# One-bank maxima, half-length value passes, a split first group, column gates, more work on POOL and a new step table in an adaLN attention block

## The reference

```python
mod = (silu(c) @ wmod)              # six vectors of 128: sa, ca, ga, sb, cb, gb
ga, gb = sign(ga) * max(|ga|, 0.25), sign(gb) * max(|gb|, 0.25)
h = layernorm(x) * (1 + ca) + sa
q, k, v = h @ Wq.T, h @ Wk.T, h @ Wv.T          # 8 heads of 16
probs = softmax(causal(q @ k.T / 4))
x = x + ga * (probs @ v)
h = layernorm(x) * (1 + cb) + sb
p = softmax(h @ gate_W.T)                       # 8 experts
scale = count(p > 0.3) * p                      # counts fall on experts 0 and 1
x = x + gb * ((sum over experts of scale * (h @ expert_W.T)) @ out_W.T)
```

## Time and profile before

| what | value |
|---|---|
| runs of the kernel before | 287.44, 288.61, 291.89 us |
| median | 288.61 us |
| time of the profiled execution | 290.65 us |
| its span, first to last instruction | 288.9 us |
| mean granted clock of TensorE | 0.892 of full speed |

### The profile page before, as it was taken

The page is one execution under the profiler, slowest core; times in us unless marked ns, Lnnn a source line. Parts: engine busy times, 40 slices in busy tenths (PEclk is TensorE's granted clock), DMA queues, the critical chain, the costliest instruction groups (busy, mean ns, idle before and its releaser), DMA issues.

```text
span 288.9 us, 6404 instructions
## 1 busy us (share of the span) xinstructions
PE 274.0 (95%) x2427; PEld 168.8 (58%) x2427; DVE 214.7 (74%) x435; ACT 194.6 (67%) x415; POOL 38.9 (13%) x72
## 2 busy tenths in 40 slices
PE   6999999989999999999999999999999999999944
PEld 2656564546564535446686766676666666666622
DVE  3769999798699979999996499997686863704033
ACT  2344576455499668859986348786768899989910
POOL 7510004002032102000110000200110101101000
PEclk9799996895799979999975599986979999899995
DMA  7200000000000000100000010000000000000000
GB/s 196 59 1 2 0 5 1 5 0 2 2 0 3 3 3 0 37 2 1 2 5 0 0 39 2 2 3 19 2 2 1 3 23 0 2 1 5 20 0 18
DMA packets 5583, 3.42 MB, mean 12 GB/s; under 512 B 457, under 2 KB 5393, under 8 KB 5553
## 3 DMA queue, kind: packets, MB, share of 16 engines
q1 hardware_dynamic: 4976, 2.50, 3.2%
q10 hardware_dynamic: 576, 0.53, 0.6%
HBM read 1.84 MB, written 1.05 MB: 10 GB/s over the span
## 4 chain that ended last, share of the span: by engine, by line
PE 68%; DVE 13%; issue 9%; ACT 6%; DMA 2%; ACTq 1%; POOL 0%; POOLq 0%; DVEq 0%
PE ctx_ps L981 18%; PE ps L944 15%; PE ps L957 14%; DVE part_max L732 10%; PE ps L996 5%; ACT probs L631 3%; PE ps L1061 3%; PE ps L965 2%; PE ps L1030 2%; DMA w_sb<-in_L_attn_Wk 2%; PE ps L1043 2%; PE ps L1050 1%; PE ps L1056 1%; PE ps L1036 1%; PE ps L1025 1%
## 5 line engine op out<-in xcount | busy, mean ns | idle before, releaser
L732 DVE TENSOR_REDUCE part_max<-ps 128x2 f32<-128x1024 f32 (+3 forms) x160 | 163.3, 1060 | 28.0 <-PE ps L965 16.0
L631 ACT ACTIVATE probs<-ps 128x512 f32<-128x512 f32 x208 | 104.1, 607 | 27.4 <-PE ps L944 26.9
L944 PE MATMUL ps<-q_stack,k_stack 50*128 50x256 f32 (+3 forms) x512 | 88.0, 337 | 0.8 <-ACT probs L631 0.2
L957 PE MATMUL ps<-k_stack,q_stack 48*128 48x512 f32 (+3 forms) x320 | 80.1, 465 | 2.0 <-DVE part_max L732 0.6
L944 PEld LDWEIGHTS ps<-q_stack,k_stack 50*128 50x128 f32 x512 | 63.0, 199 | 25.6 <-ACT probs L631 7.4
L981 PE MATMUL ctx_ps<-probs,v_aug 128*32 128x256 f32 (+3 forms) x1024 | 73.5, 427 | 0.0
L957 PEld LDWEIGHTS ps<-k_stack,q_stack 48*128 48x128 f32 x320 | 38.1, 199 | 24.4 <-DVE part_max L732 9.6
L628 ACT ACTIVATE probs<-ps 128x512 f32<-128x512 f32 (+3 forms) x96 | 40.4, 499 | 17.3 <-PE ps L944 16.9
L981 PEld LDWEIGHTS ctx_ps<-probs,v_aug 128*32 128x32 f32 x1024 | 30.7, 115 | 28.1 <-issue 9.9
L602 POOL TENSOR_SCALAR_AFFINE_SELECT probs<-probs 128x512 f32<-128x512 f32 x32 | 20.2, 635 | 169.6 <-ACT probs L631 99.3
L996 PE MATMUL ps<-piece,spread 128*128 128x512 f32 x64 | 23.0, 476 | 0.0
(11 more groups left out here) (91 smaller groups left out, 171.5 us busy)
## 6 DMA issues: line engine op xcount, KB each, us to landing
x_sb<-in_L_attn_hidden_states SPq DMA_DIRECT2D x4, 256.0 KB, 5.3
out_x<-result SPq DMA_DIRECT2D x2, 256.0 KB, 2.5
out_x<-result SPq DMA_DIRECT2D x4, 128.0 KB, 1.8
wmod<-in_L_wmod ACTq DMA_DIRECT2D x1, 384.0 KB, 5.0
q_stack<-max_row SPq DMA_DIRECT2D x16, 4.0 KB
expert_w<-in_L_ffn_expert_W SPq DMA_DIRECT2D x1, 128.0 KB, 5.5
q_stack<-max_row SPq DMA_DIRECT2D x8, 8.0 KB
w_sb<-in_L_attn_Wv SPq DMA_DIRECT2D x1, 64.0 KB
```

The source lines that it names most:

```text
L631: drained(act.activation(probs[:, :, prob_columns(b)].rearrange("p (n e) q -> p e n q", e=2)[:, e], bank.rearrange("p (n q) -> p n q", n=2 ...
L732: dve.tensor_reduce(part_max[:, n % 2, i, 2 * e:2 * e + 2, c], banks[:, :, 0:width], AX.X, ALU.max).then_inc(vec_drained, 1)
L944: last = pe.matmul(out_at, k_stack[at:at + rows, p, j * P:(j + 1) * P], q_stack[at:at + rows, p, tile * P + q0:(tile + tiles) * P], start= ...
L957: last = pe.matmul(banks[:, m, 0:width], q_stack[at:at + ROWS, p, tile * P:(tile + 1) * P], k_stack[at:at + ROWS, p, c * BANK:c * BANK + w ...
```

## The change

Seven things change together.

- `maxima`: a unit is now one bank. On chunks wider than 256 keys a unit is one head (matmul, then its two masks on the diagonal, then a reduction of 512 columns at most); on narrower ones it is two heads that share a half of the rows, side by side in one bank. The units alternate between the halves. 160 units become 288: 256 of one head and 32 of two. `PAIR_STAGES` holds the ffn alone.
- `PASS_UNITS` goes from 4 to 2: 76 passes in place of 40.
- `GROUPS`: the first group of 512 tokens becomes two of 256; there are five groups, with 40 spreads in place of 32. The loads are split and ordered anew: x in pieces of 256 tokens first, the modulation's first two vectors ahead of the other four, Wk on the SP queue, and the weights of values and experts last.
- Gates as columns: the modulation's gates are computed as columns of one element for each partition. POOL scales the rows of Wv and out_W by them before they are transposed (`scale_weights`, `gated_weights`), in place of DVE work on 128x256 elements. ACT copies the product of the experts' weights out (`expert_out`).
- More on POOL: the normalized tiles that ACT made, the add of the variance's epsilon, `context_add` of items 0 to 9, and for the last three groups both pieces of the projections (`project_wide`: ACT copies the bank to `wide`, POOL makes the high piece and the low one).
- `WARM` goes from (11, 1, 2, 8) to (8, 1, 2). `bn`, `mean_var`, `var_eps` and `rstd` have a place for each norm in place of two that alternate.
- `ORDER` is a new table of 905 letters for 725, with two new streams (T the statistics of a group, V values and gates).

The core of the diff:

```diff
-NG = S // GROUP
+GROUPS = [(0, 2), (2, 2), (4, 4), (8, 4), (12, 4)]
+SPLIT_GROUPS = 2
-PASS_UNITS = 4
-WARM = (11, 1, 2, 8)
+PASS_UNITS = 2
+WARM = (8, 1, 2)
...
-    return [("maxima", n, i, e, c) for i in range(BLOCKS[n // 2][1]) for e in range(HALF // 2)
-            for c in range(key_chunks(n))]
+    units = []
+    for i in range(BLOCKS[n // 2][1]):
+        for c in range(key_chunks(n)):
+            narrow = maxima_width(n, i, c) <= BANK // 2
+            units += [("maxima", n, i, heads, c) for heads in ([(0, 2), (1, 3)] if narrow else [(0,), (1,), (2,), (3,)])]
+    return units
...
+def by_vec_norm(s):
+    return s in (("normalize", 0), ("normalize", 1), ("normalize2", NB - 1))
+def by_vec_add(n):
+    return n >= NI - 2
...
+                    for t in range(tiles):
+                        pool.tensor_scalar(normed[:, k % 2, t, :], x_sb[:, first + t, :], mean_var[:, k, t, 0:1],
+                                           rstd[:, k, t:t + 1], ALU.subtract, ALU.mult).then_inc(pool_normed, 1)
+                elif step[0] == "project_wide":
...
+                    pool.tensor_copy(piece[0][:, g % 2, qk, :], wide[:, qk, :]).then_inc(pool_pieces, 1)
+                    pool.wait_ge(pool_pieces, pieces_until(g, qk) - 1)
+                    pool.tensor_tensor(piece[1][:, g % 2, qk, :], wide[:, qk, :], piece[0][:, g % 2, qk, :].bitcast(F32),
+                                       ALU.subtract).then_inc(pool_pieces, 1)
+                elif step[0] == "context_add" and not by_vec_add(step[1]):
...
+                    pool.tensor_tensor(part, part, ctx_norm[:, n % 2, 0:tiles, :], ALU.add).then_inc(x_added, 1)
...
+                elif step[0] == "scale_weights":
+                    pool.wait_ge(gates_ready, 1)
+                    pool.wait_ge(ffn_in, 16 * 3)
+                    for k in range(2):
+                        pool.tensor_scalar(w_sb[:, 2 + k, :], w_sb[:, 2 + k, :], gates[:, k:k + 1], None,
+                                           ALU.mult).then_inc(weights_scaled, 1)
...
-                    dve.tensor_reduce(part_max[:, n % 2, i, 2 * e:2 * e + 2, c], banks[:, :, 0:width], AX.X,
+                    dve.tensor_reduce(part_max[:, n % 2, i, heads[0]:heads[-1] + 1:2, c],
+                                      banks[:, 0, 0:len(heads) * width].rearrange("p (e k) -> p e k", k=width), AX.X,
                                       ALU.max).then_inc(vec_drained, 1)
...
-                    for m in range(2):
-                        p, at = pair_of(n, 2 * e + m)
-                        last = pe.matmul(banks[:, m, 0:width], q_stack[at:at + ROWS, p, tile * P:(tile + 1) * P],
-                                         k_stack[at:at + ROWS, p, c * BANK:c * BANK + width],
-                                         start=True, stop=c < g)
-                    if c == g:
-                        pe.wait_ge(const_ready, CONSTS["halves"])
-                        for half in range(2):
-                            for m in range(2):
-                                at = TILE * m
-                                last = pe.matmul(banks[:, m, width - P:width], ident_half[at:at + TILE, half, :],
-                                                 mask_half[at:at + TILE, half, :], start=False, stop=half == 1)
+                    for m, e in enumerate(heads):
+                        p, at = pair_of(n, e)
...
+                        last = pe.matmul(banks[:, 0, m * width:(m + 1) * width],
+                                         q_stack[at:at + ROWS, p, tile * P:(tile + 1) * P],
+                                         k_stack[at:at + ROWS, p, c * BANK:c * BANK + width],
+                                         start=True, stop=c < diagonal_chunk)
+                        if c == diagonal_chunk:
+                            pe.wait_ge(const_ready, CONSTS["halves"])
+                            for half in range(2):
+                                last = pe.matmul(banks[:, 0, (m + 1) * width - P:(m + 1) * width],
+                                                 ident_half[at:at + TILE, half, :], mask_half[at:at + TILE, half, :],
+                                                 start=False, stop=half == 1)
...
 ORDER = (
-    "AAAAMAMMMMAMMMAXXAAAMMMMMXMAAMMAAAAMXMMMMAMMAXAAMXSMAASMSMASSSSSMSMSSASSMSAMXMPMSSXAMMXMMAAMSMAAMMMS"
+    "TTAAVTMTMMMVTAAAAAAAAAVAAMMMMAAMMMMXVAXATXMMMMMMVXAMTMMMMMVAAAMMXSSAMMXSTMMXMSSASSMMXMSSMMMSPSMMSSSP"
```

More of the change, by code:

```diff
@@ L148, in key_chunks, with group_of, groups_between, columns @@
     return BLOCKS[n // 2][0] // TG + 1
[L151 to L153 removed]
+def group_of(tile):
+    return [g for g, (first, tiles) in enumerate(GROUPS) if first <= tile < first + tiles][0]
+def groups_between(first, last):
+    return range(group_of(first), group_of(last) + 1)
+def columns(g):
+    first, tiles = GROUPS[g]
+    return slice(first * P, (first + tiles) * P)
+def maxima_units(n):
+    units = []
[4 more added lines that the diff above has]
+    return units
 def token_stats(name, k):
```

475 lines of the change are left out of this document (264 added, 211 removed).

## The result

| what | before | after |
|---|---|---|
| median (runs) | 288.02 us (4) | 256.67 us (4) |
| lowest to highest | 286.74 to 291.89 | 256.57 to 257.73 |
| profiled execution, span | 290.65, 288.9 | 256.59, 254.9 |
| granted clock | 0.892 | 0.985 |

The kernel before, and some experiments on it, have slower executions beside the usual ones; ratios and intervals leave these out, while medians are over all executions.

The account below looks back on a forecast made before the run. It saw successive limits: start, DVE (19 to 145 us), PE (to 235), ACT (to 276.5). Gains 5.5 + 2 + 0 + 2 = 9.5 off 290.65 gave 281.1, a median of 279 us; range 266 to 294.

Parts of the forecast that it names:

- The start: 0 to 19 us: earlier weights, shorter path, half widths and fewer zero matmuls bring the first maximum about 5.5 us earlier (3 to 8).
- DVE is busy 114.82 of 126: it bounds, and PE waits for banks: Reading of the profile before, 19 to 145 us: DVE is the limit there and PE waits for its banks.
- I take 2 us of it back, between 0 and 8: 19 to 145 us: of 11.2 us in which DVE idles, single banks were to recover 2 us.
- some 13 us of lost column time, of which I take 3 back, with 0 and 8 as bounds: 145 to 235 us: loss from a clock of 0.85; buffers freed sooner were to recover 3 us.
- my two stages: 19 to 145 us, taken as bound by DVE, gain 2 us; 145 to 235 us, taken as bound by PE, gain 0.
- The rival that I called much faster: Single banks remove most waiting and the clock at 145 to 235 us rises to 0.96: 263 us (262 to 273), chance 0.19.
- Changes of mode: PE: 41 more switches between scores and values at 0.245 us, 10 us in all, 3.5 of it at 145 to 235 us.
- Masks in order: PE diagonals: the second head starts only with the first one's last mask; up to 10 us, taken as 2.5.
- The split of a reduction: DVE maxima: 128 more instructions at 0.07 us each cost 9.0 us, paid for by work moved off DVE.
- POOL: POOL's busy time rises from 38.9 to 54 to 123 us; it doesn't bound, so the added work is costed at 0.
- The part of ACT: 235 to 276.5 us, bound by ACT: six normalized tiles of the last blocks leave ACT, 2 us gained.
- the sign that I named for it: ACT busy for fewer than 38 us in the last 41 would show that the normalized tiles leaving it paid.

Follow-up runs that it names:

- a_late: Changed kernel with 14 more matmuls on zeros ahead of the first projection, first maximum 2.4 us later: 260.53 us, ratio 0.9133.
- b_half: Kernel before with each maxima reduction reading only half of its columns: 284.95 us, ratio 0.9646.
- b_fill128all: Kernel before with two 128-column matmuls on zeros ahead of each maxima unit of all 12 items, 8.5 us of work: 283.46 us, ratio 0.9866.
- a_pair: Changed kernel with maxima units in aligned pairs of banks again, table otherwise kept: 283.99 us, ratio 0.9805.
- a_pass4: Changed kernel with PASS_UNITS 4 in place of 2, 50 fewer changes between rows and columns: 276.58 us, ratio 0.9603.
- a_pass3: Changed kernel with PASS_UNITS 3 in place of 2, 62 passes for 76: 267.98 us, ratio 0.9352.
- a_interleave: Changed kernel with the masks of two neighbouring diagonal units behind both matmuls, alternating as before, at 53 places: 256.84 us, ratio 0.9011.
- a_dve: Changed kernel with the adds to x and all normalized tiles back on DVE: 266.20 us, ratio 0.9331.
- b_onebank: Kernel before with one-bank maxima units alone, its own table kept with each M repeated per part: 300.81 us, ratio 1.0313.
- b_newtable: Kernel before with the new order table alone, translated to its steps: 338.12 us.
- a_oldtable: Changed kernel with the old order table translated to its steps and `expert_out` computed earlier: 320.21 us.
- b_fill: Kernel before with two 512-column matmuls on zeros ahead of each maxima unit of items 0 to 5: 290.34 us, ratio 1.0076.
- b_fill128: Kernel before with two 128-column matmuls on zeros ahead of each maxima unit of items 0 to 5, 3.8 us of work: 288.99 us, ratio 1.0028.

## Why the prediction was wrong

The start was right. I gave 5.5 and it is 6.1, the first maximum at 12.70 for "near 13". Its parts were off against each other: weights 1.87 sooner (1.6 given), from there to the projection 2.76 (1.5 given), the rest 1.5 (2.3 given). a_late shows that a shift of the start reaches the end.

The step that failed is the reading "DVE is busy 114.82 of 126: it bounds, and PE waits for banks", with "I take 2 us of it back, between 0 and 8", and beside it "some 13 us of lost column time, of which I take 3 back, with 0 and 8 as bounds". I took the pauses and the clock for two things in two stages and priced each by the idle time of its own stage. The runs show one limit through both stages: PE, at a clock that keeps falling. b_half denies that DVE bounded (4 to 10 us for 66 of 215), and in it the clock stays as low, so my reading that PE waited there for DVE's banks is not the reason of the low clock either. b_fill128all speaks for the clock as a cause and not a follower; a_pair, a_pass4 and a_pass3 show that without single banks or short passes the new order loses 27, 20 and 11 us, some 9 of the 27 and 4 of the 20 by the clock and the rest by waits and by PE time that I can't place. In sum the phase from the first maximum to the last gave 24.4 us, where my two stages gave 2 and 0. The rows for it were there: the clock of 0.85 in the second stage and 0.92 in the first, over 232.2 us with a mean of 0.90, are 23 us of lost columns, about what the phase gave. Which of the seven changes holds the clock at 1.00 stays open: no run has one of them alone and the full clock.

The rival that I called much faster had the mechanism, single banks and a stage clock of 0.96, and 263 us. It was 6 us short, since it gave the clock back in one stage only and to 0.96, while it is 1.00 from the first maximum to the last. The result is also below its own range of 262 to 273.

The costs that I set against the gains are not to be seen in the time. Changes of mode: 41 more at 0.245, "3.5 here"; a_pass4 has 50 fewer and is 20 us slower. The Trainium skill says in TensorEngine Tiling (Array Packing), Key Properties, that a change of mode drains the engine; the trace agrees with 0.49 for a return trip, but what a long pass does to the others costs more. Masks in order: the row bears out that order holds, and a_interleave gives nothing for taking it away at 53 places, so the 2.5 was no cost that could be had back in this way. The split of a reduction: 0.07 given, 0 measured in a full queue, so the 9.0 us were about 3 (DVE is busy 194.58 us in the phase of maxima of a_pair, which has the reductions paired again, and 197.87 here).

POOL was right as a bound and wrong as a term: 78.9 us lies inside 54 to 123, tiles at 0.798, low pieces at 1.276 and adds at 0.46 to 0.74 lie inside theirs, high pieces at 0.610 just below their 0.64. But I cost the move as neutral on DVE's time, since I thought of it as paying for the splits; a_dve shows that it is worth 9.5 us once PE no longer wastes time. The part of ACT (2 us) can't be told apart; ACT is still busy 38.59 of 42 us in the corresponding stage, so the sign that I named for it, fewer than 38, did not come. 3.5 us fell behind the last maximum.

## What to carry to other kernels

Look at the granted clock by windows of a few microseconds before deciding which engine bounds a stage: where it stands at half level, the engine that looks full beside it may only be waiting for slow matmuls, and a mean clock of 0.90 over 232 us has to be priced at its full 23 us before shares of stages are. Leave out half of the suspected engine's work as a test: here that gave 4 to 10 us for 66. When several engines share a pool of banks, make every claim on it small and every stretch in which one engine serves none of the others short, and fit the order to that. The parts hang together: single banks alone or the table alone made the kernel slower (b_onebank, b_newtable), and each of single banks, short passes and table, taken out of the whole, cost 20 us or more (a_pair, a_pass4, a_oldtable). A quick test of the clock is to fill with matmuls on zeros: if the kernel gets faster by them, its clock is probably a cost. If it doesn't, nothing is decided, as b_fill and b_fill128 show.

## What was unexpected of the hardware

- Work that computes nothing made a kernel faster: 8.5 us of matmuls on zeros, 3.9 us less.
- Halving the reductions of DVE left the clock of PE as low as it was (0.93 and 0.83 in two stages for 0.92 and 0.85). A full DVE was not what made it fall.
- Runs of one program differ in their granted clock, from 0.881 to 0.919 in the kernel before, with times from 294.07 to 283.87 us; the four runs of the changed kernel, which hardly pauses, stay within 0.980 to 0.986 and 256.57 to 257.73.
- On POOL a normalized tile of 128 columns, one input and two scalars for each partition, takes 0.798 us, more than the cast of 512 columns (0.610). The kind of work counts there as much as its size (an add of 128 columns takes 0.460, one of 256 takes 0.735).
- A matmul of the other half of the rows started 0.47 us behind, once the masks of the first were ahead of it in the program, though the halves can run side by side; and putting them in another order did not shorten the group of four.
